# Attention inside a four-stage kernel: queries made token tile by token tile and turned per unit, their squares summed on GpSimd

## The reference

```python
q = (x @ Wq.T).reshape(b, t, N_HEADS, HEAD_DIM).transpose(0, 2, 1, 3)    # 16 heads of 128
k = (x @ Wk.T).reshape(b, t, N_KV_HEADS, HEAD_DIM).transpose(0, 2, 1, 3) # 4 heads
v = (x @ Wv.T).reshape(b, t, N_KV_HEADS, HEAD_DIM).transpose(0, 2, 1, 3)
q = _qknorm(q, q_scale)      # t * rsqrt(mean(t * t, -1) + 1e-6) * scale
k = _qknorm(k, k_scale)
scores = einsum('bhtd,bhsd->bhts', q, k) / sqrt(HEAD_DIM)   # k, v repeated for 4 heads; causal
out = einsum('bhts,bhsd->bhtd', softmax(scores), v)
y = out.transpose(0, 2, 1, 3).reshape(b, t, 2048) @ Wo.T
```

## Time and profile before

| what | value |
|---|---|
| median of 3 runs (lowest to highest) | 874.47 us (874.31 to 874.52) |
| span of the profiled execution | 873.0 us |
| median less that span | 1.5 us |
| TensorE busy | 865.5 us, 99% of the span |
| VectorE, ScalarE, GpSimd busy | 501.8, 420.0, 320.0 us |
| idle of GpSimd before the queries' factors | 137.7 us |
| idle of ScalarE before the exps | 72.6 us |

### The profile page before, as it was taken

The page is one execution under the profiler, slowest core; times in us unless marked ns, Lnnn a source line. Parts: engine busy times, 40 slices in busy tenths (PEclk is TensorE's granted clock), DMA queues, the critical chain, the costliest instruction groups (busy, mean ns, idle before and its releaser), DMA issues.

```text
span 873.0 us, 16737 instructions
## 1 busy us (share of the span) xinstructions
PE 865.5 (99%) x5617; PEld 773.3 (89%) x5620; DVE 501.8 (57%) x1360; ACT 420.0 (48%) x978; POOL 320.0 (37%) x293
## 2 busy tenths in 40 slices
PE   9999999999999999999999999999999999999998
PEld 7999878888888888889989998998997888888887
DVE  4777757333333338887688668768877433333334
ACT  3522416334334344776377557647746433434332
POOL 5211014556555564232121213212112556556552
PEclk9999999999999999999999999999999999999999
DMA  8999312111111102000000100000002111111111
GB/s 338 362 383 391 136 40 77 49 54 36 54 45 45 54 18 76 1 26 21 18 3 21 36 0 24 0 0 1 1 1 73 38 54 39 51 54 36 54 36 49
DMA packets 25554, 61.01 MB, mean 70 GB/s; under 512 B 3298, under 2 KB 10916, under 8 KB 25508
## 3 DMA queue, kind: packets, MB, share of 16 engines
q1 hardware_dynamic: 23204, 47.82, 16.1%
q0 software_dynamic: 2304, 12.58, 3.8%
HBM read 59.35 MB, written 1.05 MB: 69 GB/s over the span
## 4 chain that ended last, share of the span: by engine, by line
PE 93%; DVE 3%; ACT 1%; DMA 1%; issue 1%; POOL 0%; DVEq 0%; ACTq 0%
PE bank L1131 29%; PE bank L1655 25%; PE bank L1144 14%; PE bank L534 7%; PE bank L545 5%; PE bank L1781 4%; PE bank L1721 3%; PE bank L1157 2%; PE bank L1167 2%; DMA cv_shared<-in_wtaps 1%; PE bank L1746 1%; DVE cv_acc L421 1%; PE bank L518 1%; PE bank L1675 1%; PE bank L129 0%
## 5 line engine op out<-in xcount | busy, mean ns | idle before, releaser
L1030 DVE TENSOR_TENSOR f_h<-f_scaled,bank 128x512 f32<-128x512 f32 (+1 forms) x90 | 60.8, 676 | 179.4 <-POOL f_scaled L895 166.9
L812 ACT ACTIVATE f_h_hi<-f_h 128x512 fp32r<-128x512 f32 (+2 forms) x102 | 63.6, 624 | 186.2 <-DVE f_h L1030 186.0
L895 POOL TENSOR_TENSOR f_scaled<-f_act,f_gate_rows 128x512 f32<-128x512 f32 x80 | 102.9, 1287 | 116.3 <-ACT f_act L805 115.9
L1131 PE MATMUL bank<-f_xt_hi,f_w_lo 128*128 128x512 f32 x352 | 138.2, 393 | 0.0
L1131 PE MATMUL bank<-f_xt_hi,f_w_hi 128*128 128x512 f32 x352 | 137.8, 391 | 0.0
L1350 ACT ACTIVATE at_prob<-bank,at_sbias,at_qrs 128x512 f32<-128x512 f32 (+3 forms) x128 | 77.6, 618 | 72.6 <-DVE at_sbias L1542 72.6
L1037 DVE TENSOR_TENSOR f_h_lo<-f_h,f_h_hi 128x512 fp32r<-128x512 f32 (+2 forms) x102 | 71.8, 704 | 70.7 <-ACT f_h_hi L812 70.4
L1131 PE MATMUL bank<-f_xt_lo,f_w_hi 128*128 128x512 f32 x352 | 108.8, 390 | 0.0
L1144 PE MATMUL bank<-f_w_lo,f_h_hi 128*128 128x256 f32 (+1 forms) x352 | 99.6, 283 | 0.0
L1144 PE MATMUL bank<-f_w_hi,f_h_lo 128*128 128x256 f32 (+1 forms) x352 | 99.6, 283 | 0.0
L1144 PE MATMUL bank<-f_w_hi,f_h_hi 128*128 128x256 f32 (+1 forms) x352 | 99.3, 282 | 0.0
(11 more groups left out here) (232 smaller groups left out, 2062.8 us busy)
## 6 DMA issues: line engine op xcount, KB each, us to landing
cv_raw<-in_wconv SPq DMA_DIRECT2D x26, 512.0 KB, 6.7
cv_shared<-in_wtaps POOLq DMA_DIRECT2D x16, 768.0 KB, 7.7
f_wraw<-in_w SPq DMA_DIRECT2D x42, 256.0 KB, 2.6
xn<-in_wconv SPq DMA_DIRECT2D x14, 512.0 KB, 6.5
f_wraw<-in_w SPq DMA_DIRECT2D x42, 128.0 KB, 2.5
at_wraw<-in_wqkv SPq DMA_DIRECT2D x3, 768.0 KB, 4.4
at_oraw<-in_wo SPq DMA_DIRECT2D x4, 512.0 KB, 3.5
X<-in_x_tiles SPq DMA_DIRECT2D x2, 512.0 KB, 8.0
```

Source lines behind the costliest of these rows:

```text
L812: a.activation(h_hi[slot][0:rows, cols], h_f[half][0:rows, cols], ACT.Copy).then_inc(s["h_hi_done"], 1)
L895: g.tensor_tensor(scaled[half][:], act[half][:], gate_rows[:, half * HALF:(half + 1) * HALF], ALU.mult).then_inc(s["scaled_done"], 1)
L1030: v.tensor_tensor(h_f[half][0:rows, cols], src[half][0:rows, cols], pu[half][0:rows, cols], ALU.mult)\
L1131: mm = t.matmul((pg, pu)[gu][half][0:out_rows, :], w, x, start=q == 0, stop=q == 3 * KH - 1)
```

## The change

Queries are no longer made turned and unit by unit, but token tile by token tile for all four heads of a group: one tile is 128 tokens by 512 columns, so a group has 8 tiles, as it had 8 units. Tile n = 5 + k (`tile_at`) is made at step k behind the scores, so tiles 8 to 12 belong to the next group. ScalarE copies a tile to `q_rows` in SBUF after the exps. GpSimd squares it, sums the squares of each head by seven halvings, adds the epsilon and takes the power (`query_factors`). At the head of step k TensorE turns the query of unit k+1 from `q_rows` by four transposes into the same bank, ScalarE copies `qt_hi` at the head of its step, and VectorE makes `qt_lo` at the head of its own. The squares on ScalarE, the sums on TensorE and the added epsilon on VectorE go. Since tiles 8 and on need the next group's wq, ScalarE rounds it at step 2 and GpSimd makes its low part at step 2. The next group's first keys and values move from step 7 to step 8, and the order of their banks changes.

```diff
+        AHEAD = NQ + 1
+        HALVES = [HD >> i for i in range(1, HD.bit_length())]
+        QSQ_STEPS = 2 + len(HALVES)
...
-        KV_BANK = (3, 0, 1, 2)
+        KV_BANK = (0, 1, 2, 3)
...
+        def tile_at(k):
+            n = AHEAD + k
+            return n, n // NQ % B, n % NQ
+        def has_tile(k, last):
+            return k < NU and not (last and k + AHEAD >= B * NQ)
...
             with sp.Fori(1, NKV) as g:
+                sp.wait_ge(s["wkv_lo_done"], g)
...
+            def copy_rows(g, n, b, j, bank=Q_BANK):
+                a.wait_ge(s["q_ready"], g * B * NQ + (n + 1))
+                a.activation(q_rows[:, b, j, :], ps[bank][:], ACT.Copy).then_inc(s["q_rows_done"], 1)
             def query(g, u):
-                a.wait_ge(s["q_ready"], g * NU + (u + 1))
-                a.activation(qsq[:, u % 2, :], ps[Q_BANK][:], ACT.Square).then_inc(s["qsq_done"], 1)
+                a.wait_ge(s["qt_ready"], g * NU + (u + 1))
                 a.activation(qt_hi[:, u % 2, :], ps[Q_BANK][:], ACT.Copy).then_inc(s["qt_hi_done"], 1)
...
                     score, turn, value, ahead = steps_of(k)
+                    if ahead is not None:
+                        query(g, ahead)
                     if score is not None:
...
-                            if k <= 1 and j == 1:
-                                query(g, ahead)
...
-                    if ahead is not None and k > 1:
-                        query(g, ahead)
+                    if has_tile(k, last):
+                        copy_rows(g, *tile_at(k))
+                    if k == 2 and not last:
+                        a.wait_ge(s["w_in"], g * 16 + 32)
+                        qkv["round_q"](a, wraw)
...
-                    if k == NU - 1 and not last:
-                        qkv["round_q"](a, wraw)
...
+            def query_factors(g, n, b, j):
+                n = g * B * NQ + n
+                p.wait_ge(s["q_rows_done"], n + 1)
...
+                rows = q_rows[:, b, j, :].rearrange("p (h d) -> p h d", h=REP)
+                p.tensor_tensor(qsq[:], rows, rows, ALU.mult).then_inc(s["qsq_done"], 1)
+                for i, width in enumerate(HALVES):
+                    p.wait_ge(s["qsq_done"], n * QSQ_STEPS + (i + 1))
+                    p.tensor_tensor(qsq[:, :, 0:width], qsq[:, :, 0:width], qsq[:, :, width:2 * width], ALU.add)\
+                     .then_inc(s["qsq_done"], 1)
+                p.wait_ge(s["qsq_done"], n * QSQ_STEPS + QSQ_STEPS - 1)
+                p.tensor_tensor(qsq[:, :, 0], qsq[:, :, 0], qk_eps[:], ALU.add).then_inc(s["qsq_done"], 1)
+                p.wait_ge(s["qsq_done"], (n + 1) * QSQ_STEPS)
+                p.tensor_tensor(qrs[:, b, :, j], qsq[:, :, 0], pm["minus_half"][:, 0:REP], ALU.pow)\
                  .then_inc(s["qrs_done"], 1)
...
+                    if has_tile(k, last):
+                        query_factors(g, *tile_at(k))
+                    if k == 2 and not last:
+                        qkv["low_q"](p, wraw, g + 1)
...
             key_factors(0, (0,))
-            query_factor(0, 0)
+            p.memset(qk_eps[:], HD * QK_EPS).then_inc(s["qk_eps_ready"], 1)
+            p.wait_ge(s["qk_eps_ready"], 1)
+            for j in range(NQ):
+                query_factors(0, j, 0, j)
             key_factors(0, (1,))
+            query_factors(0, NQ, 1, 0)
+            steps(0, range(2), False)
...
-                v.wait_ge(s["qrs_done"], g * NU + (u + 1))
+                v.wait_ge(s["qrs_done"], g * NU + NQ * (u // REP + 1))
...
                     score, turn, value, ahead = steps_of(k)
+                    if ahead is not None:
+                        query_low(g, ahead)
                     if value is not None:
                         transposed_low(g, value, (0,))
...
-                    if ahead is not None and k > 1:
-                        query_low(g, ahead)
...
+            def query_rows(b, j, bank=Q_BANK):
+                tok = slice(b * C + j * P, b * C + (j + 1) * P)
+                for k in range(KH):
+                    m = triple(ps[bank][:], (xt_hi[:, k, tok], xt_lo[:, k, tok]),
+                               (wq_hi[:, k, :], wq_lo[:, k, :]), k == 0, k == KH - 1)
+                m.then_inc(s["q_ready"], 1)
+            def rows_ahead(g, k):
+                n, b, j = tile_at(k)
+                t.wait_ge(s["qt_lo_done"], g * NU + min(k + 2, NU))
+                t.wait_ge(s["q_rows_done"], g * B * NQ + n)
+                if n == B * NQ:
+                    t.wait_ge(s["wq_lo_done"], g + 2)
+                query_rows(b, j)
+            def turn_query(g, u, ready=None, last=False):
...
+                t.wait_ge(s["q_rows_done"], g * B * NQ + ready)
                 for j in range(NQ):
-                    m = t.matmul(qsum_bank(g, u)[:, j:j + 1], qsq[:, u % 2, j * P:(j + 1) * P],
-                                 ones[:, 0:1], start=True, stop=True)
-                m.then_inc(s["qsum_ready"], 1)
+                    m = t.transpose(ps[Q_BANK][:, j * P:(j + 1) * P], q_rows[:, b, j, h * HD:(h + 1) * HD], pm["ident"][:])
+                m.then_inc(s["qt_ready"], 1)
...
+                    if ahead is not None:
+                        t.wait_ge(s["qt_lo_done"], g * NU + (k + 1))
+                        turn_query(g, ahead, last=last)
                     if score is not None:
                         scores(score)
-                    if ahead is not None:
-                        query(g, ahead)
+                    if has_tile(k, last):
+                        rows_ahead(g, k)
...
-                    if k == NU - 1 and not last:
-                        t.wait_ge(s["wkv_lo_done"], g + 2)
-                        t.wait_ge(s["qt_lo_done"], g * NU + NU)
-                        keys_and_values(g + 1, (0,))
...
                     if k == NU and not last:
                         t.wait_ge(s["exp_done"], g * NU * NQ + NU * NQ)
-                        keys_and_values(g + 1, (1, 2))
+                        t.wait_ge(s["wkv_lo_done"], g + 2)
+                        keys_and_values(g + 1, (0, 1, 2))
```

More of the change, by code:

```diff
@@ L1278, in kt_bank @@
             return ps[FIRST_KT_BANK[b] if opening(g) else b]
-        def qsum_bank(g, u):
-            return FIRST_QSUM if opening(g) and u == 0 else ps[1][:, QSUM_COL:QSUM_COL + NQ]
+        def tile_at(k):
[3 more added lines that the diff above has]
+            return k < NU and not (last and k + AHEAD >= B * NQ)
         def steps_of(k):
@@ L1389, in scalar @@
             square_keys(0, (0, 1))
+            for j in range(2):
+                copy_rows(0, j, 0, j, FIRST_Q_BANK[j])
+            round_values(0, (0, 1))
+            for j in range(2, NQ):
+                copy_rows(0, j, 0, j, FIRST_Q_BANK[j])
             ln["scalar"](a, (1,))
-            round_values(0, (0, 1))
             query(0, 0)
@@ L1394, in scalar @@
             round_keys(0, 0)
+            copy_rows(0, NQ, 1, 0)
             square_keys(0, (2, 3))
@@ L1640, in vector @@
             keys_low(0, 0)
-            query_sum(0, 0)
             key_sums(0, 1)
@@ L1691, in first_keys_and_values @@
                             m.then_inc(s["kv_ready"], 1)
-            def first_query(low):
-                tok, col = slice(0, C), slice(0, HD)
-                steps = [(k, wq_hi, xt_lo) for k in range(KH)] if low else \
-                        [(k, w, xt_hi) for k in range(KH) for w in (wq_hi, wq_lo)]
-                for n, (k, w, x) in enumerate(steps):
-                    m = t.matmul(ps[Q_BANK][:], w[:, k, col], x[:, k, tok], start=not low and n == 0,
-                                 stop=low and n == len(steps) - 1)
-                if low:
-                    m.then_inc(s["q_ready"], 1)
@@ L1715, in query_sum, with first_rows @@
-            def query_sum(g, u):
-                t.wait_ge(s["qsq_done"], g * NU + (u + 1))
-                if u >= 1:
-                    t.wait_ge(s["exp_done"], g * NU * NQ + (NQ * (u - 1) + 2))
+            def first_rows(tiles, low):
+                for j in tiles:
+                    tok = slice(j * P, (j + 1) * P)
+                    steps = [(k, xt_lo, wq_hi) for k in range(KH)] if low else \
+                            [(k, xt_hi, w) for k in range(KH) for w in (wq_hi, wq_lo)]
+                    for n, (k, x, w) in enumerate(steps):
+                        m = t.matmul(ps[FIRST_Q_BANK[j]][:], x[:, k, tok], w[:, k, :], start=not low and n == 0,
+                                     stop=low and n == len(steps) - 1, skip_group_check=True)
+                    if low:
+                        m.then_inc(s["q_ready"], 1)
```

95 lines of the change are left out of this document (39 added, 56 removed).

## The result

The changed kernel takes 930.99 us (median; 930.65 to 931.55) where the kernel before took 874.39 in the same comparison (874.24 to 874.52): a ratio of 1.0648, with a 95% interval of 1.0633 to 1.0663. The forecast was 926.5, in a range of 900 to 952. The span of the profiled execution is 928.8 us, 55.8 more than before; the sum had said 52.

A forecast was written before the change was run, and what follows sets the result against it. TensorE, busy 865.5 of 873.0 us, was taken as the bound. Group terms of 38, contention 8 and clock 6 gave 52 us: 925 on the profiled span, 926.5 as median, range 900 to 952.

The forecast's parts named there:

- The new loop: Steps 2 to 6: loop through ScalarE and VectorE sums to 7.9 us, against 7.03 of TensorE; each costs 0.5 more.
- T: GpSimd's chain of factors for one token tile: 5.8 us, lower bound 4.9, upper 8.
- The opening: Start of attention: first bias needs four serial GpSimd tiles; first exp moves from 353.84 to about 371.5, step 0's end +18.1.
- Step 3: Groups 0 to 2: tile 8 waits for wq's low part behind tile 7; units 2 to 4 take 19.5 us instead of 14.8.
- Contention: Large GpSimd operations hold up VectorE's scalings: 2.7 us for each of three groups, +8; ends nothing and 15.
- the lower of the two cases: Scalings beside GpSimd: only the product gets in, 1.3 later; with halvings too, about 2.05. Steady step grows 0.6 (1.35).
- The clock: TensorE's clock falls after idling in the opening and each step 3: 1.5 us for each of four waits, +6.
- TensorE is the bound again up to the next group ... -2.1: After step 3's delay: TensorE enters unit 7 about 0.3 us after unit 6's exps, before 2.44, returning 2.1 per group.
- Group 3: Last group, making no tiles from step 3 on: 2.6 + 0.5 - 2.1 = +1.0 us.
- No contention and no fall: Rival: no contention and no fall of TensorE's clock, 874.5 + 38 = 912 us; chance 0.18.
- Dear or cheap small operations: Rivals on GpSimd: dear, T about 8, 942 us, chance 0.13; cheap, T about 3.5, 910 us, chance 0.06.
- The other side: Rival, steps 2 to 6 and opening: TensorE stays the bound as the order lets it run ahead; -11.5, 863; chance 0.03.

The follow-up runs named there:

- E1: Changed kernel with GpSimd's product, halvings and added constant per tile replaced by four small powers, equally long, factors constant: 927.1 us, 1.0604.
- E7: E3, with GpSimd also holding each tile's factors and wq's low part until that step's scalings are done; everything computed: 915.35 us, 1.0475.
- E2: Changed kernel with GpSimd's chain per tile cut to its last power (1.1 us instead of 5.5), factors constant: 899.34 us, 1.0300.
- E5: Changed kernel with GpSimd's product, halvings and constant left out for group 0's first four tiles only, their factors constant: 921.28 us, 1.0536.
- E6: Changed kernel with products of zeros keeping TensorE busy, 50 in the opening and 16 before each step 3 wait for wq: 927.42 us, 1.0612.
- E3: Changed kernel with the low part of wq made ahead of tile 7's factors in GpSimd's queue, nothing else: 926.78 us, 1.0609.
- E9: Changed kernel with VectorE making all three low parts of the transposes ahead of the maxima at step 7: 932.98 us, 1.0675.
- E10: E7 with the step 7 order of E9, everything computed: 915.06 us, 1.0466.

## Why the prediction came out right, point by point

**The new loop.** Forecast 7.9 us a step without contention. E1 and E7 show 7.90 to 7.92 in the steady steps. Right, and with it the claim that TensorE's 11.5 us of saved work go into waiting. The earlier trace rows had all the terms in them.

**T.** Forecast 5.8, measured 5.50. The seven halvings take 2.85 us less six gaps of 0.08, so 2.4, as in the sum: up to 744 ns for 256 elements, down to 201, with no penalty for strides; the product of a tile with itself is 1.04 us where nothing runs beside it, against the 1.28 of two different inputs.

**The opening.** Forecast 371.5 for the first exp, 369.19 measured. Of the 2.3 between them 0.7 is the earlier start of attention (the tiles begin at 347.15, and would at 347.84 on the clock of the kernel before, so the forecast's 348.0 was right), and 1.2 is four times the smaller T. Counted from attention's start, the first exp moved from 17.42 to 33.46, so by 16.0. E2 and E5 add what the sum did not ask: with the chain gone it is at 23.63 and 23.66, still 6.2 later than before, so 9.8 us are what the chain costs, and the rest lies hidden behind it. It belongs to the new order: in the changed kernel VectorE's maxima of unit 0 start only at 357.89, right behind the low part of unit 1's query.

**Step 3.** Forecast +6.8 for units 2 to 4, measured +6.9, along the forecast's path: tile 7's factors, the low part, TensorE's queue behind its wait, the loop. The wait was put at 5 and is 4.5. Unit 3's bias, held for 1.6 us by the same subtraction, was not in the sum and makes units 2 to 3 longer, but it lies beside the wait and not on the chain. E6, which keeps both the wait and the held bias, takes 19.55 for units 2 to 4, against the 19.5 of the sum; E3, which has neither, takes 19.68, with slower scalings and a held bias of unit 4 in their place.

**Contention.** Forecast +8, all of it on scalings. E1 puts that part at 1.8 a group, 5.5 in all. What the sum did not have are the biases. Of these unit 4's lies on the chain, 0.63 to 0.73 us instead of 0.16 in the three groups, 1.5 in all, which also stand in E6's price of the clock: 7 together. For the steady step the lower of the two cases that the forecast weighed was right: the four scalings grow by 1.28, a step by 0.55 (forecast 0.6), unit 7's by 0.8 (forecast 0.9). The Trainium skill's page "SBUF — State Buffer", section "Who interferes with whom", says that a VectorE operation with two inputs in SBUF contends with a GpSimd operation that reads SBUF. The bias has two such inputs, and this trace agrees: 1.75 us instead of 0.16. This rule was not applied to the bias in the forecast. On the other side, the forecast had asked whether a power holds the scalings up; E1 says that it does not: four scalings took 1.27 us with powers beside them.

**The clock.** Forecast +6, four falls of 1.5; E6 shows 6.7, one of 0.8 in the opening and three of 1.96, each with the 0.5 of unit 4's bias in it. The sum is near and its sharing out is not.

**The step that failed: "TensorE is the bound again up to the next group ... -2.1".** It came to +0.5 a group with contention in it, where the sum had -1.2. The forecast took TensorE's queue to be free once it had caught up. But unit 7's exps follow from the loop through ScalarE and VectorE as every other unit's: 7.90 less the query copy (0.65) and its low part (0.60) is 6.65, so the forecast's own terms allowed 0.8, and E2 has 6.59. Behind them, two waits are in TensorE's queue that were hidden before: the low parts behind the later maxima (E9, 1.2 us), and right behind these the next keys and values, which wait for the last exps. The forecast said that moving those from step 7 to step 8 "adds nothing"; E9 and E10 show that a wait for unit 7's exps stands there, which takes over as soon as the low parts are out of the way. What they leave open is whether with the keys and values back at step 7 the full 2.1 would come; that was not tried.

**Group 3.** Forecast +1.0, measured +3.3. The two first steps cost 1.8 where 2.6 was forecast. The four that follow cost 1.2, 0.5, 0.3 and 0.3, where the sum had 0.5 for one of them; without a tile to copy the forecast's loop is 7.4, but the steps take 7.72, over TensorE's values (E2). Unit 7 returned 0.8 and not 2.1.

**The rivals.** "No contention and no fall" (912) is refuted by E1 and E6, though E7 comes to 915 by removing contention. Dear or cheap small operations: T is 5.50. The other side, TensorE still the bound, needed a loop under 7.03, and it is 7.90.

The total came as near as it did because errors of both signs cancelled: 2.2 too much up to unit 2 and 0.9 in the first steps of each of groups 1 and 2, against 1.7 too little at each of three group ends and 2.3 in group 3. That cancelling is luck. It leaves 3.4 of the 4.5; the rest is rounding and a median that lies 2.2 above the span instead of 1.5, which is the 0.7 by which the profiled execution reached attention early (so the true excess up to unit 2 is 1.5).

## What to carry to other kernels

When one engine is 99% busy, taking work off it pays only as far as the loop through the others allows; add that loop up from timelines, from result to result, before counting any saving. A helper engine with half its time free can still be the bound by latency: GpSimd waited 101 us for tiles, and the length and size of its chain cost 31.7 us. Work that it does in the shadow of VectorE's SBUF-to-SBUF operations should be queued behind them, large operations above all, and an operation on two columns waits there as long as a large one; whether that costs time depends on what else ends beside it. And a gain at the end of a loop is real only after the next wait in the queue has been named.

## What was not expected of the hardware

A VectorE operation on 2 columns was held for 1.6 us by a GpSimd subtraction already running, and for 0.9 by the 1.28 us one in E3 (492.05 against 491.81); it ended with it both times.

TensorE's clock fell in places without a long idle time: in E6 its windows at 655 to 661 show 0.65 and 0.78 while its pauses there were single ones of 0.5 to 0.9 us, and the step grew by 1.2 us. The same step ran at 1.00 in the changed kernel, with TensorE busy for only 3.73 of the 6.00 us from 658 to 664. Which of such steps falls changed from kernel to kernel (unit 3 to 4 in E1, 5 to 6 in E5, E9 and E10, both in E6), which moves results of this kind by 1.4 to 2.7 us. The Trainium skill's page "TensorE: Matmul & The Clock Gate", section "Part 1", says that the clock follows how busy the array has been recently, which fits falls without any long pause; these runs do not show what decides between one kernel and the next.
